# Edge keys on GpSimd beside the degree histogram, and the powers of the variances in two parts

## The chip, the cores and the metric

The kernel runs on one core of a Trainium2 chip. The metric is the device time of one execution in microseconds, the median of several. The hardware profiler records one further execution instruction by instruction; its time is given beside its span, and all rows below are from it.

## The reference, cut to what matters

Two graph layers over 12,500 nodes with 48 features and 400,000 edges, sorted by target node:

```python
h = relu(layernorm(x))                     # rows of 48: (x - mean) / sqrt(var + 1e-5)
deg = bincount(src)                        # how often each node is a source
norm = rsqrt(deg)[src] * rsqrt(deg)[dst]   # 0 where deg is 0
x = x + relu(segment_sum(norm * h[dst], src) @ W.T + b)
h = relu(layernorm(x))
m = mlp(concat(h[src], h[dst], edge_attr)) # 112 -> 128 -> 128 -> 48
x = x + segment_sum(m, dst) / max(count(dst), 1)
```

The part at hand is only the preparation of the first layer: layer norm of x, the histogram of the sources that gives deg, and for each edge the integer keys with which the main stage of layer one builds its one-hot matrices.

## The kernel before

The edges are padded to 128 x 3136: one partition holds 3136 edges (TP), a column of 128 is a tile. Four tiles are a group (NG = 784), two tiles are a window (NW = 1568). Nodes are 98 blocks of 128 (NB). Everything is ordered by hand: each engine has its own program in a block, and semaphores order them. `link` is a helper that lets each instruction signal and makes its own engine wait for it before the next. There are stages, one after another: the preparation (to about 518 us), the main stage of layer one, which builds pieces of the adjacency matrix with `pair_l` and `tile_r` and multiplies (to about 2350 us), the node stage between the layers, and the edge stage of layer two. This is the preparation, by engine:

- SP loads the target nodes by row and by column, the sources and x; it stores each window's lowest and highest target (`ext_tab`), loads them back for every partition (`ext_bc`), stores `rel_row` out of the buffer that the second `hot_lo` takes later, fills tables with zeros, and at the end stores the scaled node rows (`g_tab`), in four parts.
- ScalarE casts sources and targets to f32 (`key_r`, `dst_rel`) and the two digits of the source (low 7 bits, the rest) to bf16 (`lo_b`, `hi_b`). Then it waits for `pow_done` and runs a loop over 98 rows of `act_in` (scale by `stat`, relu); in each step it also drains one chunk of the histogram (`keep_hist`).
- GpSimd writes constants and then waits for `pow_ask`: it raises the 98 columns of `stat` (variances) to the power -1/2 (L503), and after the histogram the four parts of the degrees `deg_is` (L507).
- VectorE splits the sources into digits, centres x (`center`, L243 to L248), asks for the powers, works out the lowest nodes of windows and groups (`base_w`, `base_col`), the group's extra blocks (`worst`, `wide`, `extra_f`) and the keys (`seg_of`, `fold_key`, `key_l`, `key_w`, `key_r`, `dst_rel`) in L575 to L604, then does a few small steps (L620 to L627), and then the histogram: 112 chunks of 28 tiles, each with two one-hot compares (L614), `hot_lo` (128 x 3584) and `hot_hi` (128 x 2744), double buffered.
- TensorE multiplies the one-hots of a chunk, 28 matmuls into `hist` (L522), and adds the chunk of two before to `src_count` (L513). It waits for ScalarE's drain of the chunk two before.

After the histogram VectorE reads the count, corrects `key_l` for crowded chunks (L647), and scales and splits the node rows in four parts.

Of the kernel before, what the change touches and what calls it, by code (L numbers as in the profile page):

```python
# [17 lines left out]
P = 128  # L18
GROUP = 4
# [3 lines left out]
SPAN = 32  # L23
WIN_TILES = 2
WIN = 11
FOLD = 11
SEG = 1152
ROUND = 12
HALF = SEG // 2
# [7 lines left out]
ALU = mybir.AluOpType  # L37
ACT = mybir.ActivationFunctionType
# [90 lines left out]
def build_gnn(nc, x, src_col, dst_col, dst_row, edge_t, w0_t, b0, w1ab, w1c, b1, w2, b2, w3, b3, out):  # L129
    N, F = out.shape  # L130
    NB = x.shape[0] // P
# [3 lines left out]
    NG = TP // GROUP  # L135
# [12 lines left out]
    NW = TP // WIN_TILES  # L148
# [26 lines left out]
    with ExitStack() as whole:  # L175
# [6 lines left out]
        def sem(name, ctx=whole):  # L182
            return ctx.enter_context(nc.semaphore(name))
# [3 lines left out]
        dst_rel = sb("dst_rel", [P, TP], F32)  # L187
# [3 lines left out]
        sched = sb("sched", [1, 3, NG], I32)  # L191
# [13 lines left out]
        half = sb("half", [P, NB], F32)  # L205
        stat = sb("stat", [P, NB], F32)
# [12 lines left out]
        key_r = sb("key_r", [P, TP], F32, keys)  # L219
        key_l = sb("key_l", [P, TP], BF16, keys)  # L220
        gw_row = sb("gw_row", [P, NS * ROUND], I32, keys)
        dst_i = sb("dst_i", [P, TP], I32, keys)
        key_w = dst_i[:, :].bitcast(F32)
# [63 lines left out]
        with ExitStack() as ctx:  # L287
# [36 lines left out]
            over = src_i[0:1, 0:NW].bitcast(F32)  # L324
            worst = src_i[0:1, 2 * NG:3 * NG].bitcast(F32)
            wide = src_i[0:1, 3 * NG:4 * NG].bitcast(F32)
            extra_i = src_i[0:1, 0:NG]
            extra_f = src_i[0:1, NG:2 * NG].bitcast(F32)
            hist = [ps(f"hist{k}", [P, NB], F32, ctx) for k in range(2)]
            most_ps = ps("most_ps", [CHUNKS, P], F32, ctx)  # L330
# [33 lines left out]
            digits_copied = sem("digits_copied", ctx)  # L364
            pow_ask = sem("pow_ask", ctx)
            pow_done = sem("pow_done", ctx)
            act_ready = sem("act_ready", ctx)
            chain = sem("chain", ctx)
            pool_chain = sem("pool_chain", ctx)
# [1 line left out]
            PIECES = NWP // 2 // READ // FOLD  # L371
            BLANK = [len([q for q in range(FOLD) if ((NS - 1) * FOLD + q) * ROUND + g * READ >= NW]) for g in range(GROUPS)]
            ZEROS = 2 + sum(BLANK) + 2 * FOLD
            assert NB % 2 == 0 and CHUNKS % 2 == 0 and NB <= CHUNKS <= P
            assert 0 < min(BLANK) and (NWP - NW) // 2 <= WK and READ * HALF <= 2 * NF and NW % READ == 0 and NS % 2 == 0
            block = ctx.enter_context(nc.Block())
# [52 lines left out]
            @block.scalar  # L429
            def _(act):  # L430
                act.sem_inc(hist_kept, 4)
                act.wait_ge(loaded, 32)
                act.copy(key_r[:, :], src_i[:, :])
                act.copy(dst_rel[:, :], dst_i[:, :]).then_inc(ids_copied, 1)
                act.wait_ge(digits_ready, 1)
                act.copy(lo_b[:, :], dst_i[:, :])
                act.copy(hi_b[:, :], src_i[:, :]).then_inc(digits_copied, 1)

                act.wait_ge(pow_done, 1)

                def keep_hist(n, k):
                    act.wait_ge(hot_used, n + 3)
                    act.activation(past_most[k][:, :], hist[k][:, :], ACT.Relu, bias=most_neg[:, 0:1],
                                   accum_out=chunk_most[:, bass.ds(n, 1)]).then_inc(hist_kept, 1)
                    act.copy(hist_got[k][:, :], hist[k][:, :]).then_inc(hist_kept, 1)

                with act.Fori(0, NB // 2) as r:
                    for k in range(2):
                        at = act_in[:, bass.ds(r * 2 + k, 1), :].rearrange("p o f -> p (o f)")
                        act.activation(at, at, ACT.Relu, scale=stat[:, bass.ds(r * 2 + k, 1)]).then_inc(act_ready, 1)  # L450
                        keep_hist(r * 2 + k, k)
                if CHUNKS > NB:
                    with act.Fori(NB // 2, CHUNKS // 2) as r:
                        for k in range(2):
                            keep_hist(r * 2 + k, k)

                def cast(n, m):
                    act.wait_ge(part_ready[m], n + 1)
                    act.copy(plane_of(n, m), part_of(n)).then_inc(plane_made[m] if m < PLANES - 1 else g_ready, 1)

                for t in range(len(PARTS) + PLANES - 1):
                    for m in range(PLANES):
                        if 0 <= t - m < len(PARTS):
                            cast(t - m, m)

            @block.gpsimd
            def _(pool):
# [32 lines left out]
                pool.tensor_scalar(ident_hi[:, :], ident_f[:, :], float(P), None, ALU.mult).then_inc(const_ready, 1)  # L500

                pool.wait_ge(pow_ask, 1)
                pool.tensor_tensor(stat[:, :], stat[:, :], half[:, :], ALU.pow).then_inc(pow_done, 1)  # L503

                for n, (a, z) in enumerate(PARTS):
                    pool.wait_ge(pow_ask, n + 2)
# [35 lines left out]
            def _(dve):  # L542
# [25 lines left out]
                dve.sem_inc(pow_ask, 1)  # L568


                dve.wait_ge(ext_loaded, 16)
                def by_pair(row):
                    return row.rearrange("p (g two) -> p two g", two=2)

                link(dve.tensor_scalar(base_w, ext_bc[:, 0, :], float(N - 1), None, ALU.min))  # L575
                link(dve.tensor_tensor(base_col[:, :], by_pair(base_w)[:, 0, :], by_pair(base_w)[:, 1, :], ALU.min))
                link(dve.tensor_copy(sched[:, 0, :], base_col[0:1, :]))

                top = by_pair(ext_bc[0:1, 1, :])
                link(dve.scalar_tensor_tensor(over, ext_bc[0:1, 1, :], float(N - 1), base_w[0:1, :],  # L580
                                              ALU.min, ALU.subtract))
                link(dve.tensor_tensor(worst, by_pair(over)[:, 0, :], by_pair(over)[:, 1, :], ALU.max))
                link(dve.tensor_tensor(wide, top[:, 0, :], top[:, 1, :], ALU.max))
                link(dve.scalar_tensor_tensor(wide, wide, float(N - 1), base_col[0:1, :], ALU.min, ALU.subtract))
                link(dve.tensor_scalar(extra_i, wide, float(P), None, ALU.add))
                link(dve.tensor_scalar(extra_i, extra_i, P.bit_length() - 1, None, ALU.logical_shift_right))
                link(dve.tensor_copy(extra_f, extra_i))
                link(dve.tensor_scalar(worst, worst, float(WIN), None, ALU.is_ge))
                link(dve.scalar_tensor_tensor(worst, wide, float(SPAN), worst, ALU.is_ge, ALU.max))
                link(dve.tensor_scalar(seg_of, key_r[:, :], 1.0 / SEG, 0.5 / SEG - 0.5, ALU.mult, ALU.add))  # L590
                link(dve.tensor_scalar(seg_of, seg_of, float(3 << 22), float(3 << 22), ALU.add, ALU.subtract))
                link(dve.scalar_tensor_tensor(key_r[:, :], seg_of, -float(SEG), key_r[:, :], ALU.mult, ALU.add))
                link(dve.tensor_tensor(fold_key.rearrange("p (w j) -> p w j", j=WIN_TILES),
                                       dst_rel[:, :].rearrange("p (w j) -> p w j", j=WIN_TILES),
                                       base_w.unsqueeze(2).to_broadcast([P, NW, WIN_TILES]), ALU.subtract))
                link(dve.scalar_tensor_tensor(fold_key, fold_key, float(FOLD), seg_of, ALU.mult, ALU.add))
                link(dve.tensor_scalar(key_l[:, :], fold_key, 1000.0, None, ALU.min))
                link(dve.tensor_scalar(seg_of, key_r[:, :], 0.5, -0.25, ALU.mult, ALU.add))
                link(dve.tensor_scalar(seg_of, seg_of, float(3 << 22), float(3 << 22), ALU.add, ALU.subtract))
                link(dve.scalar_tensor_tensor(key_w[:, :], seg_of, -2.0, key_r[:, :], ALU.mult, ALU.add))  # L600
                link(dve.tensor_scalar(key_w[:, :], key_w[:, :], 255.0, 1.0, ALU.mult, ALU.add))
                link(dve.tensor_copy(key_r[:, :], seg_of))
                by_group = dst_rel[:, :].rearrange("p (g j) -> p g j", j=GROUP)
                link(dve.tensor_tensor(by_group, by_group, base_col[:, :].unsqueeze(2).to_broadcast([P, NG, GROUP]),  # L604
                                       ALU.subtract))

                def hot_chunk(n, k):

                    dve.wait_ge(hot_used, n + 1)
# [33 lines left out]
                    dve.tensor_scalar(deg_is[:, a:z], src_count[:, a:z], 1.0, None, ALU.max).then_inc(pow_ask, 1)  # L643

                dve.wait_ge(over_made, 1)
                by_chunk = key_l[:, :].rearrange("p (n t) -> p n t", n=CHUNKS)
                link(dve.scalar_tensor_tensor(by_chunk, over_ps[:, :].unsqueeze(2).to_broadcast([P, CHUNKS, HG * GROUP]),  # L647
                                              1000.0, by_chunk, ALU.mult, ALU.max))
# [3 lines left out]
                link(dve.tensor_tensor(sched[:, 1, :], extra_f, worst, ALU.mult))  # L652
                def scale(n):
                    a, z = PARTS[n]
                    dve.wait_ge(pow_done, n + 2)
                    link(dve.scalar_tensor_tensor(deg_is[:, a:z], src_count[:, a:z], 0.0, deg_is[:, a:z], ALU.is_gt,
                                                  ALU.mult))

                    dve.tensor_tensor(part_of(n), act_in[:, a:z, :],
                                      deg_is[:, a:z].unsqueeze(2).to_broadcast([P, z - a, F]), ALU.mult  # L660
                                      ).then_inc(part_ready[0], 1)
# [1143 lines left out]
```

## Time and profile before

| | |
|---|---|
| median of 3 runs | 6568.78 us (6567.57 to 6569.43) |
| profiled execution | 6574.72 us, span of its instructions 6572.9 us |
| mean granted clock of TensorE | 0.903 |
| busy in the span | TensorE 83%, VectorE 58%, GpSimd 50%, ScalarE 26% |

Busy shares are means over stages with different limits. In the rows, a line of the timeline is: start in us, duration in us, engine, line of the kernel, operation, what is written and what is read, shapes, how many instructions are merged, and in square brackets the idle time ahead and what ended it.

### The profile page before, as it was taken

Reading aid. Unit: us, or ns where it says so; the run is one execution under the profiler, and the core shown is the slowest. Engines: PE = TensorE matmul, PEld = TensorE weight load, DVE = VectorE, ACT = ScalarE, POOL = GpSimd, SP = SyncE. Lnnn points to the kernel's source line nnn. Section 1 sums busy time; section 2 is a strip of 40 time slices with the busy share of each in tenths; the row PEclk is TensorE's granted clock in tenths of the full one; section 3 lists DMA queues with packets and bytes.
Section 4 is the critical chain, followed back from the end, with each engine's and each line's share of the span. In section 5 each row is a group of like instructions: output and inputs, shape, how many; then the busy total and the mean of one; then the engine's idle time right before and its main releaser. Section 6 shows DMA issues by size and latency. Waiting matters only on the chain. (4 is left out here: it accounts for less than half of the span.)

```text
span 6572.9 us, 150175 instructions
## 1 busy us (share of the span) xinstructions
PE 5470.7 (83%) x42716; PEld 4494.3 (68%) x42717; DVE 3814.1 (58%) x10358; ACT 1726.6 (26%) x2888; POOL 3286.2 (50%) x3414
## 2 busy tenths in 40 slices
PE   3886999999999887777788787877878878878878
PEld 3873888888888775666666666666666666666667
DVE  9999999999999654434434444343444443444433
ACT  1226555555555322111111111111111111111110
POOL 1001000000001124777777777777777777777776
PEclk9999999999999966988888889898888888888887
DMA  6005777777777743333333333333333333333333
GB/s 156 10 0 181 268 269 267 269 268 267 269 269 267 228 115 97 84 84 83 85 83 83 85 83 85 83 83 84 84 83 85 84 85 83 83 85 83 84 84 62
DMA packets 496558, 852.93 MB, mean 130 GB/s; under 512 B 267036, under 2 KB 295934, under 8 KB 496086
## 3 DMA queue, kind: packets, MB, share of 16 engines
q1 hardware_dynamic: 391495, 640.81, 30.9%
q0 software_dynamic: 104960, 210.78, 12.8%
q8 instruction: 60, 0.98, 0.1%
q14 instruction: 43, 0.35, 0.0%
HBM read 579.37 MB, written 271.78 MB: 129 GB/s over the span
## 5 line engine op out<-in xcount | busy, mean ns | idle before, releaser
L1366 POOL DMA_INDIRECT p_got<-p_tab,idx_d x3136 | 2975.3, 949 | 961.9 <-issue 863.2
L1356 DVE TENSOR_TENSOR h<-z,nb 128x512 f32<-128x512 f32 x784 | 542.4, 692 | 1606.1 <-PE z L1332 1604.5
L1352 ACT ACTIVATE h<-z,b_col 128x512 f32<-128x512 f32 x784 | 539.0, 687 | 3416.0 <-PE z L1497 3356.5
L1326 PEld LDWEIGHTS z<-ident_f,p_got 128*128 128x128 f32 x3136 | 414.7, 161 | 1406.4 <-DMA p_got<-p_tab,idx_d 1276.1
L816 PE MATMUL a_ps<-tile_r,pair_l 128*128 128x288 bf16 x6272 | 1209.7, 288 | 84.1 <-DVE tile_r L870 75.0
L1326 PE MATMUL z<-ident_f,p_got 128*128 128x128 f32 x3136 | 598.4, 323 | 804.5 <-DMA p_got<-p_tab,idx_d 804.3
L870 DVE TENSOR_SCALAR tile_r<-iota_r,key_r,dst_i 128x576 bf16<-128x576 f16 x3136 | 1174.5, 432 | 138.0 <-PE a_ps L816 112.2
L837 PE MATMUL out_ps<-gw,a_got 121*128 121x144 bf16 x13716 | 1235.6, 225 | 8.6 <-DVE big L884 6.6
L796 ACT CAST stage<-a_ps 128x576 uint16<-128x576 f32 x1568 | 1001.1, 639 | 730.1 <-PE a_ps L816 706.5
L837 PEld LDWEIGHTS out_ps<-gw,a_got 121*128 121x128 fp8e4 x13716 | 999.5, 97 | 126.8 <-issue 23.2
L1332 PEld LDWEIGHTS z<-w_sb,h 128*128 128x128 f32 x6272 | 1034.0, 234 | 56.8
L1332 PE MATMUL z<-w_sb,h 128*128 128x128 f32 x6272 | 1024.0, 317 | 0.0
L1321 PE MATMUL z<-ef,w1c_sb 128*128 128x512 f32 x1568 | 914.3, 666 | 20.3 <-DMA ef<-in_edge_t 20.3
L727 POOL DMA_INDIRECT gw<-g_tab,gw_row x144 | 153.5, 1066 | 1466.0 <-PE out_ps L837 1424.7
L1348 PEld LDWEIGHTS seg_ps<-hot_d,h 128*128 128x128 f32 x6272 | 851.1, 210 | 0.1
L1348 PE MATMUL seg_ps<-hot_d,h 128*128 128x32 f32 x6272 | 832.5, 279 | 0.1
L816 PEld LDWEIGHTS a_ps<-tile_r,pair_l 128*128 128x128 bf16 x6272 | 561.4, 114 | 214.0 <-ACT stage L796 147.0
L1531 DVE TENSOR_SCALAR_CACHE_REDUCE hot_t_d<-rel,node_id 96x512 bf16<-96x512 bf16 x784 | 581.7, 742 | 59.2 <-issue 38.8
L1555 DVE TENSOR_TENSOR big<-big,seg_ps 128x32 f32 x784 | 148.0, 189 | 695.4 <-PE seg_ps L1348 677.8
L1497 PE MATMUL z<-hot_t_d,q_win 96*128 96x512 bf16 x784 | 356.9, 455 | 0.0
L862 DVE TENSOR_TENSOR pair_l<-rows_b,key_l 128x512 bf16<-128x512 bf16 x784 | 331.0, 422 | 14.0 <-PEq L287 11.9
L522 PE MATMUL hist<-hot_hi,hot_lo 128*128 128x98 bf16 x3136 | 304.9, 270 | 0.0
(169 smaller groups left out, 3005.4 us busy)
## 6 DMA issues: line engine op xcount, KB each, us to landing
a_got<-a_tab SPq DMA_DIRECT2D x396, 576.0 KB
a_tab<-stage SPq DMA_DIRECT2D x392, 576.0 KB, 3.1
rel<-rel_row SPq DMA_DIRECT2D x392, 192.0 KB
p_got<-p_tab,idx_d POOLq DMA_INDIRECT x3136
ef<-in_edge_t SPq DMA_DIRECT2D x392, 64.0 KB
q_win<-q_tab SPq DMA_DIRECT2D x784, 24.0 KB
a_tab<-big SPq DMA_DIRECT2D x22, 567.0 KB
q_tab<-q_out SPq DMA_DIRECT2D x14, 672.0 KB, 4.7
```

The source lines that it names most:

```text
L796: act.copy(stage[k][:, i % READ, :].rearrange("p (h e) -> p h e", h=2), a_ps[:, 2 * (i % 2):2 * (i % 2) + 2, 0:PIECE]).then_inc(kept, 1)
L816: last = pe.matmul(a_ps[:, 2 * (i % 2) + h, 0:PIECE], pair_l[i // 2 % 3][:, :, i % 2 * WIN_TILES + j], tile_r[i % 4 * WIN_TILES + j][:, h ...
L837: last = pe.matmul((a_ps if tail == 2 else out_ps)[:, c, b * OUT_F:(b + 1) * OUT_F], a_got[0:ROWS, i, :].bitcast(FP8)[:, (3 * c + b) * P:( ...
L870: dve.tensor_scalar(tile_r[i % 4 * WIN_TILES + j][:, :], iota_r[:, :], key_r[:, bass.ds(t, 1)], key_w[:, bass.ds(t, 1)], ALU.is_equal, ALU ...
L1321: return pe.matmul(z1[:, :], w1c_sb[:, :], ef, start=True, stop=False, skip_group_check=True)
L1326: pe.matmul(out_tile, p_rows[:, j, :], ident_f[:, :], start=False, stop=False, is_transpose=True, skip_group_check=True)
L1332: last = pe.matmul(z2[:, j, :], h1_tile, w2_sb[:, :], start=True, stop=True)
L1348: last = pe.matmul(seg_ps[:, :], h2[:, j, :], hot[:, j, :], start=(j == 0), stop=(j == GROUP - 1))
L1352: return act.activation(h1[:, :], z1[:, :], ACT.Relu, bias=b1_col[:, 0:1])
L1356: return dve.tensor_tensor(h2[:, :, :], z2[:, :, :], nb2[:, :].unsqueeze(1).to_broadcast([P, GROUP, H]), ALU.max)
L1366: pool.indirect_dma_start(p_rows[:, j, :], None, p_tab, bass.IndirectOffsetOnAxis(idx[:, j:j + 1], 0)).then_inc(landed, 16)
L1531: dve.tensor_scalar(hot_t[s % 2][:, :], half_of(rel[s // 2], s), node_id[0:QR, 0:1], 0.0, ALU.is_equal, ALU.add, accum_out=cnt_col[s % UNR ...
```

## The change

The 24 instructions of VectorE between the centring and the small steps are taken out and written for GpSimd, behind its powers of the variances. Where VectorE used one instruction with two operations on two tensors, or a minimum of two tensors, GpSimd has two or three simpler ones, so there are 35. VectorE waits for them (`keys_ready`) only after the histogram. The powers of the variances are two instructions, for 24 and 74 columns, and ScalarE's loop is cut at the same place.

```diff
+            keys_ready = sem("keys_ready", ctx)
+            STATS = [(0, NB // 8 * 2), (NB // 8 * 2, NB)]
...
-                act.wait_ge(pow_done, 1)
...
-                with act.Fori(0, NB // 2) as r:
-                    for k in range(2):
-                        at = act_in[:, bass.ds(r * 2 + k, 1), :].rearrange("p o f -> p (o f)")
-                        act.activation(at, at, ACT.Relu, scale=stat[:, bass.ds(r * 2 + k, 1)]).then_inc(act_ready, 1)
-                        keep_hist(r * 2 + k, k)
+                for n, (a, z) in enumerate(STATS):
+                    act.wait_ge(pow_done, n + 1)
+                    with act.Fori(a // 2, z // 2) as r:
...
-                pool.tensor_tensor(stat[:, :], stat[:, :], half[:, :], ALU.pow).then_inc(pow_done, 1)
+                for a, z in STATS:
+                    pool.tensor_tensor(stat[:, a:z], stat[:, a:z], half[:, a:z], ALU.pow).then_inc(pow_done, 1)
+
+                def by_pair(row):
+                    return row.rearrange("p (g two) -> p two g", two=2)
+
+                def scaled(to, a, by, plus, then=(ALU.mult, ALU.add)):
+                    link(pool.tensor_scalar(to, a, by, plus, *then))
+
+                def rounded(to, a):
+                    scaled(to, a, float(3 << 22), float(3 << 22), (ALU.add, ALU.subtract))
+
+                def least(to, a, most):
+                    link(pool.tensor_scalar(to, a, most, None, ALU.min))
+
+                def both(to, a, b, op):
+                    link(pool.tensor_tensor(to, a, b, op))
+
+                def lower(to, a, b, gap):
+                    both(gap, a, b, ALU.subtract)
+                    link(pool.tensor_scalar(gap, gap, 0.0, None, ALU.max))
+                    both(to, a, gap, ALU.subtract)
+
+                def upper(to, a, b, gap):
+                    both(gap, b, a, ALU.subtract)
+                    link(pool.tensor_scalar(gap, gap, 0.0, None, ALU.max))
+                    both(to, a, gap, ALU.add)
+
+                gaps = fold_key[:, 0:NG]
+                pool.wait_ge(ext_loaded, 16)
+                least(base_w, ext_bc[:, 0, :], float(N - 1))
+                lower(base_col, by_pair(base_w)[:, 0, :], by_pair(base_w)[:, 1, :], gaps)
+                link(pool.tensor_copy(sched[:, 0, :], base_col[0:1, :]))
+
+                top = by_pair(ext_bc[0:1, 1, :])
+                least(over, ext_bc[0:1, 1, :], float(N - 1))
+                both(over, over, base_w[0:1, :], ALU.subtract)
+                upper(worst, by_pair(over)[:, 0, :], by_pair(over)[:, 1, :], gaps[0:1, :])
+                upper(wide, top[:, 0, :], top[:, 1, :], gaps[0:1, :])
+                least(wide, wide, float(N - 1))
+                both(wide, wide, base_col[0:1, :], ALU.subtract)
+                scaled(extra_f, wide, 1.0 / P, 0.5 + 0.5 / P)
+                rounded(extra_f, extra_f)
+                link(pool.tensor_scalar(worst, worst, float(WIN), None, ALU.is_ge))
+                link(pool.tensor_scalar(wide, wide, float(SPAN), None, ALU.is_ge))
+                both(worst, worst, wide, ALU.add)
+                least(worst, worst, 1.0)
+
+                pool.wait_ge(ids_copied, 1)
+                scaled(seg_of, key_r[:, :], 1.0 / SEG, 0.5 / SEG - 0.5)
+                rounded(seg_of, seg_of)
+                both(fold_key.rearrange("p (w j) -> p w j", j=WIN_TILES),
+                     dst_rel[:, :].rearrange("p (w j) -> p w j", j=WIN_TILES),
+                     base_w.unsqueeze(2).to_broadcast([P, NW, WIN_TILES]), ALU.subtract)
+                link(pool.tensor_scalar(fold_key, fold_key, float(FOLD), None, ALU.mult))
+                both(fold_key, fold_key, seg_of, ALU.add)
+                least(key_l[:, :], fold_key, 1000.0)
+                scaled(fold_key, key_r[:, :], 0.5, -0.25)
+                rounded(fold_key, fold_key)
+                link(pool.tensor_scalar(key_w[:, :], fold_key, -2.0, None, ALU.mult))
+                both(key_w[:, :], key_w[:, :], key_r[:, :], ALU.add)
+                scaled(key_w[:, :], key_w[:, :], 255.0, 1.0)
+                link(pool.tensor_scalar(seg_of, seg_of, -float(HALF), None, ALU.mult))
+                both(key_r[:, :], fold_key, seg_of, ALU.add)
+                by_group = dst_rel[:, :].rearrange("p (g j) -> p g j", j=GROUP)
+                both(by_group, by_group, base_col[:, :].unsqueeze(2).to_broadcast([P, NG, GROUP]), ALU.subtract)
+                pool.sem_inc(keys_ready, 1)
...
-                dve.wait_ge(ext_loaded, 16)
...
-                link(dve.tensor_scalar(base_w, ext_bc[:, 0, :], float(N - 1), None, ALU.min))
-                link(dve.tensor_tensor(base_col[:, :], by_pair(base_w)[:, 0, :], by_pair(base_w)[:, 1, :], ALU.min))
...
-                link(dve.scalar_tensor_tensor(key_r[:, :], seg_of, -float(SEG), key_r[:, :], ALU.mult, ALU.add))
...
-                link(dve.tensor_tensor(by_group, by_group, base_col[:, :].unsqueeze(2).to_broadcast([P, NG, GROUP]),
-                                       ALU.subtract))
...
                 dve.wait_ge(over_made, 1)
+                dve.wait_ge(keys_ready, 1)
...
-                    dve.wait_ge(pow_done, n + 2)
+                    dve.wait_ge(pow_done, n + 3)
```

## Rows read from the trace of the kernel before

**Rows 1.** The page: the span, and VectorE's busy tenths in 40 slices of it.
```profile
span 6572.9 us, 150175 instructions
DVE  9999999999999654434434444343444443444433
```

**Rows 2.** Timeline of the preparation, VectorE (DVE) and GpSimd (POOL).
```profile
48.34 0.98 DVE L575 TENSOR_SCALAR big<-dst_i 128x1568 f32<-128x1568 f32 x1
48.34 16.92 POOL L503 TENSOR_TENSOR stat<-stat,half 128x98 f32<-128x98 f32 x1 [36.61 <-DVEq L568]
...
62.85 3.42 DVE L592 SCALAR_TENSOR_TENSOR key_r<-big,key_r 128x3136 f32<-128x3136 f32 x1
...
66.31 3.42 DVE L593 TENSOR_TENSOR big<-dst_rel,big 128x3136 f32<-128x3136 f32 x1
...
89.28 0.15 DVE L620 TENSOR_SCALAR row_of<-row_of 128x1 f32<-128x1 f32 x1
```

**Rows 3.** The line of the histogram's compares: min/median/max in ns, first and last start in us.
```profile
L614 DVE TENSOR_TENSOR hot_lo<-digits,lo_b x112: 2006/2014/2026, 90.8 to 472.1; 128x3584 bf16<-128x3584 bf16 x112
...
L614 DVE TENSOR_TENSOR hot_hi<-digits,hi_b x112: 1567/1576/1581, 92.7 to 474.1; 128x2744 bf16<-128x2744 bf16 x112
```

**Rows 4.** Busy us of PE, PEld, DVE, ACT, POOL over the histogram; granted clock, DMA share, GB/s.
```profile
90.70:475.70 385.00, 335.22 (x3330) 309.19 (x3330) 384.73 (x224) 85.70 (x428) 0.00 (x0) 1.00 0.12 27
```

**Rows 5.** Timeline: the main stage's first instruction on VectorE.
```profile
518.09 0.43 DVE L862 TENSOR_TENSOR pair_l<-rows_b,key_l 128x512 bf16<-128x512 bf16 x1 [11.85 <-PEq L287]
```

**Rows 6.** GpSimd's groups by shape: busy us, mean ns, idle us before them.
```profile
L1311 POOL TENSOR_TENSOR big<-big x10 | 18.6, 1864 | 0.0
...
L1306 POOL TENSOR_TENSOR x<-x,h_blk 128x336 f32 x10 | 8.9, 893 | 0.0
...
L507 POOL TENSOR_TENSOR deg_is<-deg_is,half 128x24 f32<-128x24 f32 x2 | 8.3, 4167 | 415.9 <-DVE deg_is L643 415.9
...
L736 POOL COPY scan<-scan 1x512 f32<-1x512 f32 x1 | 0.6, 601 | 0.1
L500 POOL TENSOR_SCALAR ident_hi<-ident_f 128x128 bf16<-128x128 f32 x1 | 0.5, 548 | 0.1
...
L736 POOL COPY scan<-scan 1x256 f32<-1x256 f32 x1 | 0.4, 388 | 0.1
```

**Rows 7.** The line of the store of rel_row: its start, and us to landing.
```profile
L399 SPq DMA_DIRECT2D rel_row<-hot_lo x1: 459/459/459, 32.6 to 32.6; - x1
...
DMA to landing us min/median/max: 9.0/9.0/9.0
```

**Rows 8.** Timeline of the main stage, ahead of GpSimd's scans and beside them.
```profile
2097.00 0.42 DVE L862 TENSOR_TENSOR pair_l<-rows_b,key_l 128x512 bf16<-128x512 bf16 x1
...
2098.70 0.42 DVE L862 TENSOR_TENSOR pair_l<-rows_b,key_l 128x512 bf16<-128x512 bf16 x1
...
2139.55 1.48 POOL L735 TENSOR_TENSOR scan<-scan 1x783 f32<-1x783 f32 x1
2139.56 1.65 DVE L870 TENSOR_SCALAR tile_r<-iota_r,key_r,dst_i 128x576 bf16<-128x576 f16 x1
...
2145.07 1.89 POOL L735 TENSOR_TENSOR scan<-scan 1x776 f32<-1x776 f32 x1
2145.18 2.06 DVE L862 TENSOR_TENSOR pair_l<-rows_b,key_l 128x512 bf16<-128x512 bf16 x1
```

**Rows 9.** The line of tile_r: min/median/max in ns, first and last start in us.
```profile
L870 DVE TENSOR_SCALAR tile_r<-iota_r,key_r,dst_i x3136: 410/425/1940, 518.4 to 2235.2; 128x576 bf16<-128x576 f16 x196
```

**Rows 10.** The node stage: two timeline rows, and the line of the second.
```profile
2358.33 1.97 POOL L1311 TENSOR_TENSOR big<-big 128x1008 f32<-128x1008 f32 x1 [195.62 <-DVE agg L1242]
2358.61 2.05 DVE L1235 TENSOR_TENSOR total<-total,big 128x336 f32<-128x336 f32 x1
...
L1235 DVE TENSOR_TENSOR total<-total,big x14: 507/509/2054, 2356.6 to 2515.4; 128x336 f32<-128x336 f32 x14
```

**Rows 11.** Windows over GpSimd's scans in the main stage (columns as in rows 4).
```profile
2136.97:2163.24 26.27, 15.46 (x151) 12.40 (x150) 26.27 (x31) 7.33 (x12) 24.02 (x26) 0.93 0.52 173
```

More of the change, by code:

```diff
@@ L326, in build_gnn @@
             wide = src_i[0:1, 3 * NG:4 * NG].bitcast(F32)
-            extra_i = src_i[0:1, 0:NG]
             extra_f = src_i[0:1, NG:2 * NG].bitcast(F32)
@@ L445, in keep_hist @@
                     act.copy(hist_got[k][:, :], hist[k][:, :]).then_inc(hist_kept, 1)
-                with act.Fori(0, NB // 2) as r:
-                    for k in range(2):
-                        at = act_in[:, bass.ds(r * 2 + k, 1), :].rearrange("p o f -> p (o f)")
-                        act.activation(at, at, ACT.Relu, scale=stat[:, bass.ds(r * 2 + k, 1)]).then_inc(act_ready, 1)
-                        keep_hist(r * 2 + k, k)
+                for n, (a, z) in enumerate(STATS):
+                    act.wait_ge(pow_done, n + 1)
+                    with act.Fori(a // 2, z // 2) as r:
+                        for k in range(2):
+                            at = act_in[:, bass.ds(r * 2 + k, 1), :].rearrange("p o f -> p (o f)")
+                            act.activation(at, at, ACT.Relu, scale=stat[:, bass.ds(r * 2 + k, 1)]).then_inc(act_ready, 1)
+                            keep_hist(r * 2 + k, k)
                 if CHUNKS > NB:
@@ L568, in _ @@
                 dve.sem_inc(pow_ask, 1)
-                dve.wait_ge(ext_loaded, 16)
-                def by_pair(row):
-                    return row.rearrange("p (g two) -> p two g", two=2)
-                link(dve.tensor_scalar(base_w, ext_bc[:, 0, :], float(N - 1), None, ALU.min))
-                link(dve.tensor_tensor(base_col[:, :], by_pair(base_w)[:, 0, :], by_pair(base_w)[:, 1, :], ALU.min))
-                link(dve.tensor_copy(sched[:, 0, :], base_col[0:1, :]))
-                top = by_pair(ext_bc[0:1, 1, :])
@@ L580, in _ @@
[L580 to L591, printed above, removed]
@@ L592, in _ @@
-                link(dve.scalar_tensor_tensor(key_r[:, :], seg_of, -float(SEG), key_r[:, :], ALU.mult, ALU.add))
[L593 to L602, printed above, removed]
@@ L603, in _ @@
-                by_group = dst_rel[:, :].rearrange("p (g j) -> p g j", j=GROUP)
-                link(dve.tensor_tensor(by_group, by_group, base_col[:, :].unsqueeze(2).to_broadcast([P, NG, GROUP]),
-                                       ALU.subtract))
                 def hot_chunk(n, k):
```

## The prediction

> **What bounds the kernel now.** I read the page first: VectorE is full to nine tenths in the first slices, the preparation, and half idle afterwards [rows 1]. The change touches nothing later, so the question is what sets the preparation's end. The timeline of its first half [rows 2] shows one engine without a gap: VectorE centres the rows until 48.3 us, works out keys and lowest nodes from 48.34 us to the first small step at 89.28 us, and the histogram follows 1.5 us later. By its line [rows 3] the histogram is 112 chunks of two compares with medians of 2.014 and 1.576 us, the first from 90.8 us. The windows row [rows 4] has VectorE busy for 384.73 of 385.00 us while TensorE works 335.22 us and GpSimd nothing: TensorE follows, VectorE paces. The last compare starts at 474.1 us [rows 3] and the main stage's first at 518.09 us [rows 5]; the 44 us between are a chain of small steps and a store that the change leaves alone. So a microsecond taken from or added to VectorE before 475 us moves the end by one. GpSimd sits idle for 415.9 us in that stretch [rows 6], which is the room that the new work goes to.
>
> **What is removed.** The 24 instructions from L575 to L604 run back to back from 48.34 to 89.28 us (the start of L620) [rows 2]: 40.9 us. The small steps after them (1.5 us to the first compare) stay, so the histogram starts at about 49.8 us. Two other things could hold it there. The store that frees one compare buffer is issued at 32.6 us and lands after 9.0 us [rows 7], at 41.6 us: no wait. ScalarE, which must drain chunk 0 before chunk 2 goes to TensorE, now waits for powers of variances. Their whole instruction took 16.92 us [rows 2]; of its 98 columns the first part has 24, and 24 columns took 4.167 us [rows 6]. So part one is ready at 52.5 us, before chunk 0 can be counted (49.8 + 3.6 for its compares + about 3 for its matmuls, some 56 us). Part two, 74 columns, takes the remaining 12.8 us and ends near 65.3 us; it is first wanted at chunk 24, 24 x 3.4 us later (384.73 / 112 a chunk). Cost nothing; undivided it would have held ScalarE until 65.3 us, some 9 us. Gain so far: 40.9 us.
>
> **What is added on GpSimd.** Counted in the diff, 35 instructions. Two-tensor ones: five of 3136 columns, one of 1568, eight of 784, together 23,520 columns. Tensor-with-constants ones: nine of 3136, two of 1568, nine of 784, together 38,416 columns. One copy of 784. They start after the powers, at 65.3 us, and are wanted only after the histogram. SP's queue gets nothing new; on GpSimd the powers of degrees stand behind them, wanted after the histogram too. Hidden, if they cost VectorE nothing. That is the question.
>
> **Do they cost VectorE anything?** The trace of before has two places where GpSimd's elementwise work runs beside VectorE's. In the scans of the main stage [rows 8] VectorE's tile_r starts at 2139.56 us, 0.01 us after a GpSimd tensor_tensor of 1.48 us, and takes 1.65 us, where its median is 0.425 [rows 9]. A pair_l compare, with two bf16 inputs in SBUF like the histogram's two, starts inside a GpSimd tensor_tensor of 1.89 us and takes 2.06 us, against 0.42 us at 2097.00 us. In the node stage [rows 10] an f32 tensor_tensor of VectorE takes 2.05 us beside a GpSimd one of 1.97 us; the median of its line is 0.509. VectorE stands still until GpSimd's instruction is through. The powers differ: an L592 of two SBUF inputs takes 3.42 us while the power runs (48.34 to 65.26 us), as L593 does after it [rows 2].
>
> So each of the 35 instructions will hold the compares for about the time in which it streams, and all 35 fall into the stretch that VectorE paces. What one costs, from [rows 6]: two-tensor, 1008 columns in 1.864 us and 336 in 0.893, so 1.445 ns a column and 0.41 us fixed. Copy: 512 columns in 0.601 us and 256 in 0.388, so 0.83 ns and 0.18 fixed. Tensor-with-constant stands there once, 128 columns in 0.548 us. Its slope has two ends: 0.83 ns if it streams like a copy, and 2.91 ns if its fixed part is a copy's. Between them I take the fixed part of the other arithmetic form, 0.41 us: (0.548 - 0.408) / 128 = 1.09 ns.
>
> Does VectorE lose the streaming part only, or more? The scans answer. Groups of one pair_l and four tile_r come 1.70 us apart undisturbed (2097.00 to 2098.70 us), and the six from 2136.97 to 2163.24 us took 26.27 us [rows 8, 11] where 10.2 would do: 16.1 us lost. GpSimd's prefix sums there (tensor_tensor forms of 784 - 2^n columns, n from 0 to 9, and one of 784) come to 7,601 columns, 11.0 us by the slope above, with copies of 1,023 columns in all (0.85) and three casts of 784 (1.96): 13.8 us. The difference over its 25 instructions is 0.09 us each.
>
> **The sum.** Lost by VectorE: 23,520 x 1.445 ns = 34.0 us; 38,416 x 1.09 ns = 41.9; the copy 0.65; 35 x 0.09 = 3.2; together 79.7 us. Gained 40.9. Net 38.8 us longer. The profiled execution would go from a span of 6572.9 us (its own time 6574.7, so 1.8 around it) to about 6611.7; it lay 5.9 us over the median, and 6568.8 + 38.8 = **6607.6 us**, which I call 6608. With the ends of the one unknown price: at 0.83 ns 31.9 in place of 41.9, net 28.8, 6598; at 2.91 ns 111.8, net 108.7, 6677.
>
> TensorE costs nothing beside this: a chunk is 335.22 / 112, some 3.0 us of matmuls, and a chunk with two GpSimd instructions in it lasts 3.6 us plus two streams. Even at half clock (6 us a chunk) it would only matter beside the short ones; in the scans, busy 15.46 of 26.27 us, it was granted 0.93 [rows 11]. GpSimd itself ends early enough: 80 us of streams, 14 of fixed parts and a wait of up to one compare (2 us) for each of 35, from 65.3 us on, is at most about 230 us; the histogram now ends past 500.
>
> The Trainium skill (GPSIMD Engine Reference, § 3.1 Elementwise) gives a GpSimd add of 2048 f32 columns 4497 ns, 2.2 ns a column, where the rows here have 1.445; by the page the two-tensor term would be 51.6 us and the time 6625. Its § 4.1 calls one-input work on GpSimd "roughly line-rate", which no row here shows for this form; it would give the lower end, 6598.
>
> **The rivals.**
> *Nothing is held.* The histogram's second operand is a few values repeated over a large shape, and no row has GpSimd beside exactly that. If its reads don't meet GpSimd's, the 40.9 us stay: 6528. Against it: pair_l also repeats its second operand, and took 2.06 us [rows 8]. The point from which it decides: VectorE losing less than 41 us, which is 0.51 of what I count. 12 in 100.
> *Partly held, about even.* The loss is 28 to 54 us, for instance because GpSimd's large instructions let compares through as the powers do. The time would be within 13 us of before. 5 in 100.
> *Constants forms are dear.* Five of the nine long ones apply two operations; near 2.91 ns, about 6677. One row of 128 columns can't exclude it. 10 in 100.
> *GpSimd starves.* Compares stand back to back; if GpSimd only rarely got in, its 91 us (76.6 of streams, 14 fixed) would come after the histogram's end at 434.7 us, at the new wait ahead of L647: 91 - 40.9, or 6619. Against it: in the scans it got in behind a single tile_r each time. 5 in 100.
> *The powers hold too.* If the 16.9 us of powers, which now run beside compares, held them: 17 us more, 6625. [Rows 2] say otherwise for a two-input L592. The Trainium skill (SBUF — State Buffer, § Who interferes with whom) has VectorE with two SBUF inputs and a GpSimd reader exclude each other for the whole instruction, which would make this so; by that rule the scans and the node stage agree and L592 doesn't. 3 in 100.
>
> **How the numbers follow.** The forecast has 65 in 100; with dear constants, starving and powers, slower has 83. Faster 12, same 5; by same I mean within 0.2%, 13 us, about what a measurement of this kernel tells from no change. The range leaves out the faster case and little else: from a little under the cheap end, 6586 us, to the dear end, 6680.
>
> **What would show it.** Right: L614 starts near 49.8 us; its compares have a group mean well over 2.0 and 1.6 us, single ones up to 4 to 7 us beside GpSimd's, their sum up by some 80 us on 402 (112 x 3.59); after GpSimd's last, they are back at 2.01 and 1.58; GpSimd's 3136-column forms last 3.9 to 5 us plus at most one compare; the main stage starts near 557 us. ScalarE waits for no power. Wrong, if compares beside GpSimd keep 2.01 us (main stage at 477 us), or if the constants forms take 9 us (main stage near 627).

## The result, and the profile after

The changed kernel takes 6634.8 us (median of 5 runs, 6632.1 to 6638.5) against 6568.8: 66.0 us longer, a ratio of 1.0101 with a 95% interval of 1.0089 to 1.0113. Slower, as forecast, and inside the range (6586 to 6680), but 27 us above the 6608 that the sum gave.

The page after, with the lines that answer to [rows 1]:

```profile
span 6634.0 us, 150190 instructions
...
DVE  9998999999999834343443444434344344434443
```

Two lines of the kernel after, the compares and the main stage's `pair_l` (min/median/max in ns, first and last start in us), answering to [rows 3] and [rows 5]:

```profile
L645 DVE TENSOR_TENSOR hot_lo<-digits,lo_b x112: 2009/2015/9847, 50.0 to 539.2; 128x3584 bf16<-128x3584 bf16 x112
...
L645 DVE TENSOR_TENSOR hot_hi<-digits,hi_b x112: 1573/1577/9379, 52.0 to 541.1; 128x2744 bf16<-128x2744 bf16 x112
```
```profile
L894 DVE TENSOR_TENSOR pair_l<-rows_b,key_l x784: 404/417/2076, 585.2 to 2300.2; 128x512 bf16<-128x512 bf16 x196
```

The histogram starts at 50.0 us, 40.7 earlier, and the medians of its compares are those of before. But single ones last up to 9.8 us, and the whole goes from 50.0 to 542.7 us, 492.6 us where before it took 384.9: 107.7 us lost. The main stage starts 67.1 us later (585.2 against 518.1). Everything of the 66 us has come about by then. (The spans of the two profiled executions differ by 61.1 us only; that of before lay 5.9 us over its median, as the prediction says.)

The windows of the kernel after (columns as in [rows 4]): the powers, GpSimd's short instructions, its long ones, the rest of the histogram.

```profile
48.50:65.60 17.10, 11.05 (x100) 10.32 (x101) 16.48 (x15) 2.76 (x13) 17.03 (x2) 1.00 0.88 149
65.60:141.70 76.10, 44.13 (x413) 40.81 (x410) 76.10 (x28) 11.25 (x56) 74.34 (x23) 0.84 0.53 119
141.70:250.80 109.10, 32.76 (x300) 30.37 (x300) 109.10 (x20) 8.02 (x40) 107.91 (x14) 0.52 0.17 42
250.80:502.00 251.20, 218.00 (x2163) 201.10 (x2164) 251.06 (x147) 57.45 (x286) 0.00 (x0) 0.99 0.00 0
```

VectorE counts as busy throughout, 109.10 of 109.10 us, yet begins 20 compares in the third window, where 251 us of the fourth hold 147. A held instruction looks busy; the count of instructions in the window shows that it is not at work. TensorE was granted 0.52 there, near its lower level of 1.2 GHz; it had worked 44.13 of the 76.10 us of the window before and worked 32.76 of these 109.10. VectorE never waited for it, so that cost nothing.

The timeline of the kernel after shows who holds whom:

```profile
162.24 7.65 DVE L645 TENSOR_TENSOR hot_hi<-digits,hi_b 128x2744 bf16<-128x2744 bf16 x1
...
170.41 8.10 POOL L520 TENSOR_TENSOR big<-big 128x3136 f32<-128x3136 f32 x1
171.76 8.19 DVE L645 TENSOR_TENSOR hot_hi<-digits,hi_b 128x2744 bf16<-128x2744 bf16 x1
178.59 9.35 POOL L517 TENSOR_SCALAR key_l<-big 128x3136 bf16<-128x3136 f32 x1
179.87 8.08 DVE L645 TENSOR_TENSOR hot_lo<-digits,lo_b 128x3584 bf16<-128x3584 bf16 x1
187.88 1.57 DVE L645 TENSOR_TENSOR hot_hi<-digits,hi_b 128x2744 bf16<-128x2744 bf16 x1
```

GpSimd's tensor_tensor at 170.41 us first waits for the compare at hand, to 171.8 us. The next compare is started at 171.76 and ends at 179.95. If its own 1.57 us lie at the end, it stood from 171.8 to 178.4 us, which is 6.6 us and about what GpSimd's instruction has left (6.7, to 178.51). Then the sides change again.

### The profile page after: what moved, and what is told of

The parts are those of the page before. It is cut to its first block and busy times, and to the rows that moved or that the text cites. A ratio compares the mean times of both kernels' runs of the same rounds, so it can differ in the third digit from the quotient of the medians.

```text
span 6634.0 us, 150190 instructions
## 1 busy us (share of the span) xinstructions
PE 5494.1 (83%) x42716; PEld 4518.9 (68%) x42717; DVE 3875.5 (58%) x10334; ACT 1724.4 (26%) x2888; POOL 3460.0 (52%) x3450
```

## The experiments

They ran on two other chips, on which the kernel before takes 7651 us (first four runs below) and 7599 us (last four), TensorE being granted 0.82 on average. So each ratio is against the runs of before on the same chip, and the expectations' absolute times as differences to 6569. The preparation's own instructions last within 2% as long there.

**Only the powers in two parts.**

```diff
-                pool.tensor_tensor(stat[:, :], stat[:, :], half[:, :], ALU.pow).then_inc(pow_done, 1)
+                for a, z in STATS:
+                    pool.tensor_tensor(stat[:, a:z], stat[:, a:z], half[:, a:z], ALU.pow).then_inc(pow_done, 1)
```

> The kernel before with the powers of the variances in two parts and nothing moved. Theory (the cost lies in GpSimd's reads holding the compares): ScalarE is free long before its first chunk at 94 us in this order, so the time is that of before, 6569 us, within 0.1%. Rival (part of the 66 us comes from the cut powers or from ScalarE's loop in two pieces): 5 us or more above before.

Measured, as a ratio to the kernel before with its 95% interval: 1.0001 (0.9992 to 1.0010). The cut and ScalarE's two loops are no part of the 66 us.

**Without the 14 long instructions.**

```diff
                 pool.wait_ge(ids_copied, 1)
-                scaled(seg_of, key_r[:, :], 1.0 / SEG, 0.5 / SEG - 0.5)
...
-                both(by_group, by_group, base_col[:, :].unsqueeze(2).to_broadcast([P, NG, GROUP]), ALU.subtract)
+                link(pool.memset(key_r[:, :], -1.0))
+                link(pool.memset(key_w[:, :], 1.0))
```

> The changed kernel without its 14 instructions of 3136 columns (the keys are left out; three memsets give them fixed values, so the main stage adds zeros). Theory: the 14 long ones cost the compares 78 us of the 108 lost (from 138.6 to 252.5 us the compares did 36 us of work in 114), the 21 short ones 30 us, memsets nothing: 30 - 41, so 6558 us, faster than before. Rival (VectorE loses by any work of GpSimd beside it): the three memsets of some 2.7 us cost too, 6566. Rival (a lowered clock of TensorE makes much of the loss): less is won back, since the short ones alone already lowered it: 6580 or more.

Measured: 0.9985 (0.9976 to 0.9994), 10.6 us faster than before (interval 5 to 18); the theory had 10.8. By the medians the long ones made 77 us of the loss (66.0 + 10.6; 74 with the changed kernel's 63.6 us further down) and the short ones 30. The traces agree: here the compares go from 49.6 to 463.1 us, 28.6 us longer than before's 384.9, which leaves 79 us for the long ones, and the main stage starts at 505.6 us, 13.0 us earlier than in the run above. So the difference lies ahead of the main stage; that it adds zeros here doesn't matter to it. The rival of the lowered clock (6580 or more) is out, and that of costly memsets (6566) lies outside the interval.

**Writing in place of reading.**

```diff
+                for _ in range(42):
+                    link(pool.memset(fold_key, 0.0))
```

> The same, with 42 memsets of 128x3136 f32 on GpSimd in place of the 14 left out: GpSimd is as busy beside the compares as in the changed kernel (some 113 us) but reads nothing. Theory (GpSimd's reads hold compares with two inputs): as short_only, 6558 us, and compares beside a memset last 2.0 and 1.6 us. Rival (any work of GpSimd holds them): 110 us more, near 6670.

Measured: 0.9988 (0.9979 to 0.9997), 8.9 us faster than before, not to be told from the run above. In the kernel with the 42 memsets GpSimd is busy with them from 144.13 us on; first the timeline, then the line of `hot_hi` from 144 to 250 us:

```profile
144.13 36.12 POOL L557 MEMSET big<- 128x3136 f32 x13
144.13 2.03 DVE L633 TENSOR_TENSOR hot_lo<-digits,lo_b 128x3584 bf16<-128x3584 bf16 x1
146.07 1.58 DVE L633 TENSOR_TENSOR hot_hi<-digits,hi_b 128x2744 bf16<-128x2744 bf16 x1
```
```profile
L633 DVE TENSOR_TENSOR hot_hi<-digits,hi_b x31: 1580/1592/1601, 146.1 to 249.1; 128x2744 bf16<-128x2744 bf16 x31
```

A GpSimd that only writes holds nothing: none of these 31 compares is longer than 1.601 us. The Trainium skill (SBUF — State Buffer, § Who interferes with whom) says the same: a VectorE instruction with two SBUF inputs contends with a GpSimd instruction that reads SBUF, not with one that only writes it; these rows agree.

**GpSimd's 35 after the histogram.**

```diff
                 pool.wait_ge(ext_loaded, 16)
+                pool.wait_ge(count_made, 1)
```

> The changed kernel, all 35 instructions kept but made to wait for the histogram's end, with VectorE waiting for them: nothing runs beside them, so their own prices stand in the trace. Theory (VectorE lost just the time in which they streamed, 108 us, and the fixed parts were hidden): they take 108 us and some 10 us of fixed parts and hand-overs, so 6569 - 41 + 118 = 6646 us, between 6636 and 6656. Rival (they are as short as my sum had them, 91 us, and contention made both sides slower): 6619. Forms: if the price is by operation, add-and-subtract takes 10 us or more on 3136 columns and multiply-and-add some 3 us.

Measured: 1.0133 (1.0118 to 1.0149), 103.5 us slower than before; expected were 77, by the rival 50. Neither came true: the 35 take longer alone than either had them. GpSimd works from 440.65 to 583.5 us, 142.8 us, and less the 40.7 us gained that is 102. Its groups by shape (busy us, mean ns, idle before) in this kernel are the prices with nothing beside them:

```profile
L511 POOL TENSOR_SCALAR big<-big 128x3136 f32<-128x3136 f32 x2 | 21.6, 10808 | 0.2
...
L559 POOL TENSOR_SCALAR big<-big 128x3136 f32<-128x3136 f32 x1 | 8.1, 8147 | 0.1
...
L520 POOL TENSOR_TENSOR big<-big 128x3136 f32<-128x3136 f32 x1 | 6.8, 6784 | 0.1
...
L520 POOL TENSOR_TENSOR src_i<-src_i,big 1x784 f32<-1x784 f32 x2 | 3.7, 1845 | 0.2
...
L511 POOL TENSOR_SCALAR dst_i<-dst_i 128x3136 f32<-128x3136 f32 x1 | 2.8, 2807 | 0.1
...
L524 POOL TENSOR_SCALAR big<-big 128x784 f32<-128x784 f32 x1 | 2.2, 2170 | 0.1
```

The first is the rounding (add, subtract), the second a multiply, the fifth a multiply-and-add, the last a maximum. Of 140.0 us of such instructions the compares lost 107.7. The other 32 us, about 0.9 an instruction, are not only a fixed part: beside the multiply of 9.80 us from 160.53 us in the changed kernel, the compare started at 162.24 us was through at 169.89 and so, if its 1.57 us lie at the end, began them at 168.3, 2.0 us before GpSimd's end. Reckoned in the same way, the compares beside the roundings of 12.03 and 12.45 us began 2.9 us before their end, those beside a two-tensor instruction or a multiply-and-add within 0.2 us of it.

**Other forms for the same results.**

```diff
-                    scaled(to, a, float(3 << 22), float(3 << 22), (ALU.add, ALU.subtract))
+                    scaled(to, a, 1.0, float(3 << 22))
+                    scaled(to, to, 1.0, -float(3 << 22))
...
-                link(pool.tensor_scalar(fold_key, fold_key, float(FOLD), None, ALU.mult))
+                scaled(fold_key, fold_key, float(FOLD), 0.0)
```

> The changed kernel with GpSimd's forms alone exchanged: each multiply becomes multiply-and-add of 0, each rounding (add and subtract in one) becomes two multiply-and-adds; tensor_tensor and min stay. By the prices measured alone (8.14 us for a multiply, 10.8 for a rounding, 2.81 for multiply-and-add on 3136 columns). Theory (VectorE is held while GpSimd's instruction streams, by its form): a multiply held it 6 us and a multiply-and-add 2.6, three of them give back 10 us; a rounding held it 7.8 us, two multiply-and-adds hold it 5.2, two of them give back 5: 15 to 17 us less than the changed kernel, +47 on before. Rival (the hold goes by columns, whatever the form): the three more instructions make it slower than the changed kernel by some 8 us.

Beside it ran the changed kernel once more:

> The changed kernel itself, as the ground against which the next three are read on this chip: 61 to 67 us above before.

Measured: the changed kernel 1.0085 (1.0069 to 1.0101), 63.6 us over before; with other forms 1.0071 (1.0054 to 1.0087), 53.0 us over before. The intervals overlap, so the times alone don't settle it; the traces do. Groups of the compares, first with the changed kernel's forms, then with the others:

```profile
L645 DVE TENSOR_TENSOR hot_lo<-digits,lo_b 128x3584 bf16<-128x3584 bf16 x112 | 266.3, 2378 | 0.6 <-DVE node_id L658 0.4
L645 DVE TENSOR_TENSOR hot_hi<-digits,hi_b 128x2744 bf16<-128x2744 bf16 x112 | 244.8, 2186 | 0.0
```
```profile
L646 DVE TENSOR_TENSOR hot_lo<-digits,lo_b 128x3584 bf16<-128x3584 bf16 x112 | 265.4, 2370 | 0.5 <-DVE node_id L659 0.4
L646 DVE TENSOR_TENSOR hot_hi<-digits,hi_b 128x2744 bf16<-128x2744 bf16 x112 | 229.5, 2049 | 0.0
```

511.1 against 494.9 us: 16.2 us less held, within the 15 to 17 expected, and with three instructions more; the main stage starts 14.9 us earlier (570.4 against 585.3). At the same number of columns the form sets the hold, and the rival by columns is out.

**The compares' first input in PSUM.** The tensors of the kernel lie in SBUF, the on-chip memory that the rows above read and write; PSUM is the one that takes TensorE's sums (`hist`, `src_count`). ScalarE copies the table of digits there once.

```diff
+            digits_ps = ps("digits_ps", [P, P * GROUP // 2], F32, ctx)
...
+                act.wait_ge(const_ready, 1)
+                act.copy(digits_ps[:, :], digits[:, :, :].rearrange("p d j -> p (d j)").bitcast(F32))
...
-                        values = digits[:, 0:width, :].unsqueeze(1).to_broadcast(shape)
+                        values = digits_ps[:, :].bitcast(BF16).rearrange("p (d j) -> p d j", j=GROUP)[:, 0:width, :].unsqueeze(1).to_broadcast(shape)
```

> The changed kernel with the digits table, the compares' first input, held in PSUM: each compare has one input in SBUF, all else as changed. Theory (a compare is held because its two SBUF inputs need the read path that GpSimd uses): GpSimd's instructions hold nothing, compares keep 2.0 and 1.6 us beside them and the whole 40.9 us gain shows: before less 41. Rival (GpSimd's reads hold any VectorE instruction): slower than before by 60 or more, as the changed kernel. Rival (a bf16 input from PSUM is read one column at a time): every compare nearly doubles, 3.7 and 2.9 us, some 340 us slower than before, and beside GpSimd's work no longer than elsewhere.

And the same placement in the kernel before:

> The kernel before with the digits table in PSUM, nothing moved. If the compares are as fast from PSUM as from SBUF, the time of before within 0.1%; what it differs by is the price of the placement itself, to be taken off the run above.

Measured: 0.9938 (0.9924 to 0.9952), 48.9 us faster than before and 112.5 faster than the changed kernel; the placement alone 1.0004 (0.9995 to 1.0014). The changed kernel with the table in PSUM, first the compares' lines, then the timeline beside one of GpSimd's long instructions, then the line of `pair_l`:

```profile
L648 DVE TENSOR_TENSOR hot_lo<-digits_ps,lo_b x112: 2010/2010/2025, 50.0 to 430.5; 128x3584 bf16<-128x3584 bf16 x112
...
L648 DVE TENSOR_TENSOR hot_hi<-digits_ps,hi_b x112: 1573/1573/1577, 52.0 to 432.4; 128x2744 bf16<-128x2744 bf16 x112
```
```profile
140.51 6.92 POOL L523 TENSOR_TENSOR big<-big 128x3136 f32<-128x3136 f32 x1
141.27 1.57 DVE L648 TENSOR_TENSOR hot_hi<-digits_ps,hi_b 128x2744 bf16<-128x2744 bf16 x1
142.76 2.01 DVE L648 TENSOR_TENSOR hot_lo<-digits_ps,lo_b 128x3584 bf16<-128x3584 bf16 x1
144.69 1.57 DVE L648 TENSOR_TENSOR hot_hi<-digits_ps,hi_b 128x2744 bf16<-128x2744 bf16 x1
146.19 2.01 DVE L648 TENSOR_TENSOR hot_lo<-digits_ps,lo_b 128x3584 bf16<-128x3584 bf16 x1
```
```profile
L897 DVE TENSOR_TENSOR pair_l<-rows_b,key_l x784: 404/417/1927, 476.9 to 2328.5; 128x512 bf16<-128x512 bf16 x196
```

No compare is longer than 2.025 us, GpSimd's tensor_tensor lasts 6.92 us where alone it took 6.78, and the main stage starts at 476.9 us, 41.2 us earlier than in [rows 5] and 40.5 earlier than with the same placement in the kernel before on the same chip (517.4): the whole gain, and the fastest kernel of this study against its before. That the median is 48.9 us lower and not 41 is inside its interval (36 to 58 us); what makes the rest, if it is more than noise, no run here shows.

## Why the prediction was right, point by point

- *What bounds.* Right: VectorE paces to the histogram's end, and what it loses moves the main stage one for one (107.7 - 40.7 = 67.0; the main stage came 67.1 us later).
- *What is removed.* Right: 40.7 us measured, 40.9 predicted. The histogram began at 50.05 us (49.8 predicted) with no wait for the stored buffer. ScalarE had its first power at 53.1 us and drained chunk 0 without delay. The powers, 17.1 us, held the compares for nothing that matters: the compares between 50.05 and 64.22 us last 1.57 to 2.16 us. The rival by which they would hold is out.
- *Does GpSimd hold the compares?* Right, and shown by both sides: with GpSimd's reads gone (memsets) or with one input of the compares moved to PSUM, nothing is held. The rivals "nothing is held", "partly held" and "starves" are out; GpSimd ended at 250.7 us (the prediction had 230 at most, by its low prices), and no instruction of it took over 1.9 us more than alone, which is one compare at most.
- *What it costs.* This is the step that was mis-sized: lost 79.7 us by the sum, 107.7 measured. Both prices per column were too low, and I took too little as hidden. The two-tensor price, 1.445 ns and 0.41 us fixed, came from one row that reads the same tensor twice (L1311) and one that reads two (L1306) [rows 6]. The line through two unlike forms has the slope of neither. Two-tensor instructions alone: 1.845 us at 784 columns and 6.784 at 3136, so 2.10 ns and 0.20 fixed. L1306 (336 columns, 0.893 us) lies on that line; L1311 (1008 columns) would be 2.32 us on it and took 1.864. The 14 took 49.4 us alone where the sum has 34.0 of streams and 5.7 fixed. Here the 2.2 ns a column of the Trainium skill (GPSIMD Engine Reference, § 3.1 Elementwise) was nearer than my rows.
- The constants forms took 89.8 us alone where the sum has 41.9 and 8.2. The one row for them, 0.548 us at 128 columns, could have a slope from 0.83 to 2.91 ns, and I chose near the low end by lending it the fixed part of another form, itself wrong. Alone the slow ones cost 2.54 ns a column ((8.147 - 2.170) / 2352), near the upper end, with 0.18 us fixed; only multiply-and-add runs at 0.90 (2.807 / 3136). Roundings cost 3.4, above my upper end. The "roughly line-rate" of the Trainium skill (GPSIMD Engine Reference, § 4.1) holds, among the forms with constants here, for multiply-and-add alone. "Dear constants" was half right: dear in price, but part of that price holds nobody, and the main stage started at 585 us where that rival had 627 and the forecast 557.
- The errors went against each other: 140.0 us of GpSimd's instructions instead of 90.7, of which 0.77 was lost instead of 0.88. That the time still fell inside the range owes something to this.
- *TensorE.* Right that it cost nothing, though its clock fell to 0.52 where I had 0.93 from the scans.

## What to carry to other kernels

Before work goes from VectorE to an idle GpSimd, look for a place in the trace where both read SBUF at once. If VectorE's instruction grows from 0.4 to 2 us there, idle GpSimd time is no room for work that reads. What made it room here was to give the bounding VectorE compare only one SBUF input, by a table of 1 KB a partition in PSUM. That is shown for this compare only: `tile_r`, which has one table and two per-partition columns in SBUF, was held as well (1.65 us in [rows 8] where its median is 0.425). A price per column needs two rows of the same form; a line through two forms fits neither.

## What the runs showed of the hardware that was not expected

- On GpSimd the price of a tensor-with-constants instruction hangs on the operations, not their number: on 3136 f32 columns multiply-and-add 2.8 us, a multiply or a minimum alone 8.1, add-and-subtract 10.8 (a maximum was seen on 784 columns, 2.2 us, as the other single operations there).
- The slow forms on 3136 columns release VectorE 2.0 us (a multiply or a minimum) or 2.9 us (a rounding) before their end; what they do in that time no run here shows.
- A VectorE compare with one bf16 input in PSUM and one in SBUF is as fast as with both in SBUF (medians of 2.010 and 1.573 us against 2.014 and 1.576).
